# Another order of statements in the step loops of an attention and int8 feed-forward kernel

## The reference

```
x = x + attn(layernorm(x), Wq, Wk, Wv, Wo)
x = x + ffn(layernorm(x), weight, w_scale, bias)

attn: q = rope(x @ Wq); k = rope(x @ Wk); v = x @ Wv
      scores = q k^T / 8, causal; out = softmax(scores) v; out @ Wo
ffn:  scale = max(|x|)/127 per token; q = round(x/scale)
      (q @ weight^T) * scale * w_scale + bias, as float16
```

## Time and profile before

| | us |
|---|---|
| median of 3 runs | 748.71 |
| lowest and highest run | 747.67, 748.79 |
| the profiled execution | 747.3 |
| its span | 745.1 |
| PE busy, PE's weight loads busy | 702.5, 588.8 |
| VectorE, ScalarE, GpSimd busy | 658.8, 634.4, 557.9 |
| mean granted clock of TensorE | 0.992 of full |

### The profile page before, as it was taken

The page is one execution under the profiler, slowest core; times in us unless marked ns, Lnnn a source line. Parts: engine busy times, 40 slices in busy tenths (PEclk is TensorE's granted clock), DMA queues, the critical chain, the costliest instruction groups (busy, mean ns, idle before and its releaser), DMA issues.

```text
span 745.1 us, 22980 instructions
## 1 busy us (share of the span) xinstructions
PE 702.5 (94%) x8014; PEld 588.8 (79%) x8014; DVE 658.8 (88%) x1697; ACT 634.4 (85%) x1317; POOL 557.9 (75%) x525
## 2 busy tenths in 40 slices
PE   4889999999999999999999999999999999999993
PEld 3667887878888888888888888888888888888872
DVE  6858999998889989888899898988989988988996
ACT  4778998888889989898889889898898889888883
POOL 4585887787878898787797798778697898777502
PEclk9999999999999999999999999999999999999996
DMA  8233343343334433333333343333433333232300
GB/s 266 57 98 102 73 118 87 83 114 86 87 87 97 85 92 78 87 92 82 86 92 92 94 96 80 87 90 81 96 85 97 87 94 87 67 71 62 86 2 29
DMA packets 56992, 65.80 MB, mean 88 GB/s; under 512 B 12592, under 2 KB 43824, under 8 KB 56880
## 3 DMA queue, kind: packets, MB, share of 16 engines
q1 hardware_dynamic: 53808, 53.85, 30.1%
q0 software_dynamic: 3072, 10.49, 5.1%
HBM read 16.06 MB, written 2.10 MB: 24 GB/s over the span
## 4 chain that ended last, share of the span: by engine, by line
PE 76%; DVE 11%; ACT 8%; issue 3%; DMA 1%; POOL 0%; ACTq 0%; POOLq 0%; DVEq 0%
PE x_bank L644 23%; PE t_bank L788 19%; PE o_bank L807 13%; PE s_bank L767 7%; PE s_bank L768 6%; ACT prob L1098 5%; DVE neg_max L1465 3%; DVE s_bank L1473 2%; PE ot_bank L858 2%; DVE probT L1453 2%; PE s_bank L773 2%; PE t_bank L644 1%; ACT neg_max L1096 1%; DVE value_lo L1323 1%; ACT probT L989 1%
## 5 line engine op out<-in xcount | busy, mean ns | idle before, releaser
L1110 ACT ACTIVATE probT<-t_bank 128x512 f16<-128x512 f32 x320 | 192.1, 600 | 46.3 <-PE t_bank L788 46.3
L1453 DVE SCALAR_TENSOR_TENSOR probT<-t_bank,probT 128x512 f16<-128x512 f32 x320 | 215.2, 686 | 13.5 <-ACT probT L1110 11.4
L788 PE MATMUL t_bank<-ident,prob 128*128 128x128 f32 x1280 | 192.1, 277 | 1.1 <-DVE value_lo L1323 0.7
L1473 DVE CUSTOM_DVE_ANT_0 s_bank<-s_bank,mask_row,score_unit 128x512 f32<-128x512 f32 (+1 forms) x256 | 174.6, 683 | 3.5 <-PE s_bank L768 1.8
L807 PE MATMUL o_bank<-value_hi,probT 128*128 128x65 f16 x2560 | 157.8, 194 | 5.1 <-DVE probT L1453 3.3
L1098 ACT ACTIVATE prob<-s_bank,neg_max 128x512 f32<-128x512 f32 (+1 forms) x256 | 161.2, 645 | 1.2 <-DVE neg_max L1473 1.0
L807 PEld LDWEIGHTS o_bank<-value_hi,probT 128*128 128x128 f16 x2560 | 137.7, 97 | 25.9 <-DVE probT L1453 18.6
L788 PEld LDWEIGHTS t_bank<-ident,prob 128*128 128x128 f32 x1280 | 144.0, 141 | 15.3 <-issue 2.3
L767 PE MATMUL s_bank<-kT,qT 128*128 128x384 f16 (+3 forms) x512 | 140.4, 301 | 11.1 <-ACT prob L1098 7.5
L807 PE MATMUL o_bank<-value_lo,probT 128*128 128x64 f16 x1280 | 141.7, 192 | 0.0
L768 PE MATMUL s_bank<-kT,qT 128*128 128x384 f16 (+3 forms) x512 | 139.3, 299 | 0.0
(11 more groups left out here) (146 smaller groups left out, 1151.3 us busy)
## 6 DMA issues: line engine op xcount, KB each, us to landing
...
qT<-query_pair SPq DMA_DIRECT2D x256, 64.0 KB, 2.1
kT<-key_pair SPq DMA_DIRECT2D x128, 64.0 KB, 2.0
...
```

The source lines that it names most:

```text
L788: last = nc.tensor.transpose(t_bank[B % TURN_BANKS][:, h * P:(h + 1) * P], prob[:, B % PROBS, h, :], ident[:, :])
L1110: nc.scalar.activation(turned_half[B % TURNED][HI], t_bank[B % TURN_BANKS][:, :], ACT.Copy, scale=PROB_SCALE).then_inc(probT_hi, 1)
L1453: nc.vector.scalar_tensor_tensor(out=turned_half[B % TURNED][LO], in0=t_bank[B % TURN_BANKS][:, :], scalar=PROB_SCALE, in1=turned_half[B % ...
L1473: nc.vector.tensor_tensor_reduce(bank, bank, mask_row[:, SEQ - n:SEQ], score_unit[:, 1, s % KV_HEADS:s % KV_HEADS + 1], UNBOUNDED, ALU.add ...
```

## The change

The same statements stand in another order in the step loops of the five engines. The arguments of each, the number of instructions, tiles, buffers and semaphores are the same. On SyncE the queries of pair 1 are placed before those of pair 0, the loads of output weights stand between them, and stores stand before place_keys. GpSimd rotates and loads in another order. On PE scores(s, 10) stands before turn(s, 4), attend(s, 2) behind turn(s, 5), turn(s, 7) before turn_output(s, 1). On ScalarE keep_high(s + 1, 1) stands later, and keep_raw(s + 2, 0) and keep_probT(s, 6) are exchanged with their neighbours. On VectorE several statements of the middle and the feed-forward part move.

```diff
--- before.py
+++ after.py
@@ -384,18 +384,18 @@
             swap_halves(1, 1)
             for s in range(STEPS):
                 swap_key_halves(s + 2)
+                if s == WO_CHUNKS:
+                    load_ffn_rows()
+                place_queries(s + 1, 1)
                 if s % 2 == 0:
                     load_wo(s + 2)
                     load_wo(s + 3)
                 place_queries(s + 1, 0)
-                place_queries(s + 1, 1)
                 swap_halves(s + 2, 0)
                 swap_halves(s + 2, 1)
-                if s == WO_CHUNKS:
-                    load_ffn_rows()
-                place_keys(s + 2)
                 for f in biased_tiles(s - 1):
                     store_tile(f)
+                place_keys(s + 2)
 
             for f in biased_tiles(STEPS - 1):
                 store_tile(f)
@@ -595,26 +595,26 @@
                 rotate_second(s + 1, 1)
                 rotate_first(s + 1, 1)
                 rotate_sum(s + 1, 1)
+                scale_inputs(scaled_tiles(s))
                 keep_low(s + 1, 0)
                 keep_low(s + 1, 1)
+                rotate_keys_first(s + 2)
                 done_rstd(s)
+                rotate_keys_second(s + 2)
+                split_group_weights(s + 3)
+                rotate_keys_sum(s + 2)
                 for f in biased_tiles(s):
                     add_bias(f)
                     add_residual(f)
-                split_group_weights(s + 3)
-                scale_inputs(scaled_tiles(s))
                 if s % 2 == 1:
                     keep_wo_low(s + 1)
                     keep_wo_low(s + 2)
-                rotate_keys_second(s + 2)
-                rotate_keys_first(s + 2)
-                load_group_weights(s + 5)
-                rotate_keys_sum(s + 2)
-                keep_keys_low(s + 2)
                 for f in normalised_tiles(s):
                     normalise_done(f)
+                keep_keys_low(s + 2)
+                rotate_first(s + 2, 0)
                 rotate_second(s + 2, 0)
-                rotate_first(s + 2, 0)
+                load_group_weights(s + 5)
                 rotate_sum(s + 2, 0)
 
             normalise_done(LOOP_TILES)
@@ -914,35 +914,35 @@
             for s in range(STEPS + 1):
                 turn(s, 0)
                 scores(s, 4)
+                sum_next_weights(s)
                 turn_output(s - 1, 3)
-                sum_next_weights(s)
                 project_keys(s + 2)
                 scores(s, 5)
                 scores(s, 6)
                 attend(s, 0)
                 turn(s, 1)
+                turn_quant(done_tile(s))
                 turn(s, 2)
-                turn_quant(done_tile(s))
                 scores(s, 7)
                 out_product(s - 1, 3)
                 turn_output(s, 0)
                 scores(s, 8)
                 turn(s, 3)
                 attend(s, 1)
+                ffn_product(done_tile(s))
                 scores(s, 9)
-                ffn_product(done_tile(s))
+                scores(s, 10)
                 turn(s, 4)
-                attend(s, 2)
-                scores(s, 10)
                 project(s + 2, 0)
                 turn(s, 5)
+                attend(s, 2)
                 attend(s, 3)
+                turn(s, 6)
                 attend(s, 4)
-                turn(s, 6)
                 out_product(s, 0)
+                turn(s, 7)
                 turn_output(s, 1)
                 attend(s, 5)
-                turn(s, 7)
                 attend(s, 6)
                 turn(s, 8)
                 out_product(s, 1)
@@ -1196,10 +1196,12 @@
                 exponentials(s, 1, 1)
                 keep_probT(s, 0)
                 exponentials(s, 1, 2)
+                keep_oT(s - 1, 3)
+                exponentials(s, 1, 3)
                 if s % 2 == 1:
                     keep_wo(s + 1)
-                keep_oT(s - 1, 3)
-                exponentials(s, 1, 3)
+                if s % 2 == 1:
+                    keep_wo(s + 2)
                 keep_raw_keys(s + 2)
                 keep_high(s + 1, 0)
                 keep_probT(s, 1)
@@ -1207,22 +1209,20 @@
                 keep_probT(s, 2)
                 exponentials(s, 2, 1)
                 keep_oT(s, 0)
-                keep_high(s + 1, 1)
                 exponentials(s, 2, 2)
                 keep_probT(s, 3)
+                keep_high(s + 1, 1)
                 exponentials(s, 2, 3)
                 keep_probT(s, 4)
                 exponentials(s, 3, 0)
                 exponentials(s, 3, 1)
+                keep_probT(s, 5)
                 keep_raw(s + 2, 0)
-                keep_probT(s, 5)
+                keep_probT(s, 6)
                 exponentials(s, 3, 2)
-                keep_probT(s, 6)
                 exponentials(s, 3, 3)
                 keep_oT(s, 1)
                 keep_probT(s, 7)
-                if s % 2 == 1:
-                    keep_wo(s + 2)
                 round_tile(done_tile(s + 1))
                 keep_probT(s, 8)
                 to_whole(done_tile(s + 1))
@@ -1230,10 +1230,10 @@
                 keep_high_keys(s + 2)
                 keep_raw(s + 2, 1)
                 keep_oT(s, 2)
+                for h in range(GROUP_HEADS):
+                    exponentials(s + 1, 0, h)
                 if s == STEPS - 1:
                     root(2, slice(LOOP_TILES, LOOP_TILES + 2))
-                for h in range(GROUP_HEADS):
-                    exponentials(s + 1, 0, h)
 
             normalise_done(LOOP_TILES + 1)
             root(3, slice(LOOP_TILES + 2, TOK_TILES))
@@ -1585,62 +1585,62 @@
             for s in range(STEPS + 1):
                 if s < STEPS:
                     normalise_output(s - 1, 3)
+                batch_statistics(s, 0)
                 maxima(s, 3)
-                maxima(s, 4)
                 if s % KV_HEADS == 2:
                     for f in maximum_tiles(s):
                         absolute_maximum(f)
+                maxima(s, 4)
                 group_scales(s + 2, o_bank, 0)
                 keep_probT_low(s, 0)
+                batch_statistics(s, 1)
                 keep_oT_low(s - 1, 3)
                 maxima(s, 5)
                 invert_sums(s, 0)
                 maxima(s, 6)
+                keep_quant(done_tile(s))
                 normalise_output(s, 0)
-                keep_quant(done_tile(s))
-                batch_statistics(s, 0)
+                keep_probT_low(s, 1)
                 if s == STEPS:
                     finish_root(2, slice(LOOP_TILES, LOOP_TILES + 2))
                     offset_means(2, slice(LOOP_TILES + 1, LOOP_TILES + 2))
-                keep_probT_low(s, 1)
                 maxima(s, 7)
+                add_product(s - 1, 3)
                 keep_probT_low(s, 2)
-                add_product(s - 1, 3)
                 maxima(s, 8)
-                maxima(s, 9)
-                batch_statistics(s, 1)
                 batch_statistics(s, 2)
                 scale_product(done_tile(s))
+                maxima(s, 9)
                 keep_probT_low(s, 3)
+                batch_statistics(s, 3)
+                group_maxima(s + 3)
                 keep_probT_low(s, 4)
+                keep_oT_low(s, 0)
                 maxima(s, 10)
-                group_maxima(s + 3)
-                keep_oT_low(s, 0)
-                batch_statistics(s, 3)
+                keep_probT_low(s, 5)
                 invert_sums(s, 1)
                 normalise_output(s, 1)
-                keep_probT_low(s, 5)
-                invert_scales(scaled_tiles(s))
                 keep_probT_low(s, 6)
                 add_product(s, 0)
+                batch_aggregate(s)
+                invert_scales(scaled_tiles(s))
                 keep_oT_low(s, 1)
                 keep_probT_low(s, 7)
-                last_statistics(s, 0)
-                batch_aggregate(s)
                 add_product(s, 1)
                 invert_sums(s, 2)
+                keep_probT_low(s, 8)
                 normalise_output(s, 2)
                 if s % KV_HEADS == 3:
                     for f in maximum_tiles(s):
                         absolute_maximum(f)
-                keep_probT_low(s, 8)
                 keep_probT_low(s, 9)
                 maxima(s + 1, 0)
+                last_statistics(s, 0)
                 keep_oT_low(s, 2)
-                last_statistics(s, 1)
                 maxima(s + 1, 1)
                 invert_sums(s, 3)
                 maxima(s + 1, 2)
+                last_statistics(s, 1)
                 if s == STEPS - 1:
                     normalise_output(s, 3)
                     aggregate(LOOP_TILES, LOOP_TILES + 2, TOK_TILES)
```

## The result

| | before | after |
|---|---|---|
| median of 7 runs each, us | 748.51 | 751.05 |
| lowest and highest | 747.67, 748.98 | 750.25, 751.76 |
| ratio, 95% interval | | 1.0034 [1.0023, 1.0046] |
| the profiled execution, its span | 747.3, 745.1 | 750.7, 748.8 |

The changed kernel is 2.5 us slower, a third of a percent: above the 0.2% that a measurement can tell. The forecast, no change at 748.9 us, has the time within its range and the side wrong; "slower" had a chance of 0.29. Three runs among those behind this document, of 1006 and 2463 us (the kernel before) and 3964 us (a variant), stand far outside the rest and are in no ratio or median.

The account below looks back on a forecast made before the run. TensorE was taken to bound the kernel, with little wait in reach; steps +0.3, batch steps +0.3, step 0 +0.3 and early steps -0.5 gave about +0.4 us, stated as 748.9 us on a median of 748.71, range 744.5 to 753.0.

Parts of the forecast that it names:

- What bounds the kernel, and how much can change: TensorE bounds it, with some 40 us of load waits; the order reaches only a small wait in a step's middle.
- waits for probT "near 17" us: Sign of a right forecast: TensorE's waits for VectorE's low halves of turned probabilities stay near 17 us.
- The sum: Steps +0.3, batch steps +0.3, step 0 +0.3, early steps -0.5: about +0.4 us, given as 748.9 us.
- The middle of step 17: From scores(s,9) to attend(s,7): TensorE gains 0.10 us, lost again before out_product(s,1) with 0.03 on top.
- Steps: 32 x (0.00 to 0.03) = 0 to +1.0 us, taken as +0.3: All 32 steps: each keeps its length or grows by up to 0.03 us through the oT chain before out_product(s,1).
- the slower rival: oT chain slips 0.15 us more per step before out_product(s,1), if keep_oT starts after 429.75: 4.8 us, 753.5; chance 0.24.
- The faster rival: oT chain keeps up, so TensorE keeps its 0.10 to 0.17 us a step: 3.5 us, 745.2 us; chance 0.28.
- Early steps' out_product(s,0), whose oT half comes sooner, -0.5: In the early steps out_product(s,0) gets its oT half sooner, gaining 0.5 us.
- Step 0, +0.3: Step 0, already late with its queries, may wait once, 0 to 1 us, taken as +0.3.
- Batch steps, +0.3: Steps 8, 16, 24: aggregation before keep_oT_low(s,1) costs at most 0.37 us each; +0.3 us in all.
- GpSimd ... free: GpSimd's key and query rotations move by up to a microsecond at no cost, since it idles and has 0% of the chain.
- The late-queries rival: Query transfers landing over 4.9 us after issue cost 0.5 us in each of 16 even steps: 8 us, 757; chance 0.05.

Follow-up runs that it names:

- the run with the order turned round: Changed kernel with core engines in former order in the last two steps, plus keep_oT_low(s,1) ahead of batch_aggregate and invert_scales on VectorE; 750.13 us, 1.0025.
- the three core lists: TensorE, ScalarE and VectorE in the changed order, SyncE and GpSimd as in the kernel before; 749.71 us, 1.0026.
- the former ScalarE list: Kernel before with only SyncE's and GpSimd's lists changed, TensorE, ScalarE and VectorE as before; 749.23 us, 1.0010.

## Why the prediction was right and wrong

**What bounds the kernel, and how much can change: right.** The waits at the start and the end of a step are the same to 0.01 us in step 17 (0.68, 0.51 and 0.35 against the earlier trace rows), the time stayed within the range, and the gap before attend(s,5) is gone. One sign contradicted the text's own count: waits for probT "near 17" us cannot stand beside a gap of 0.17 us that goes in each of 32 steps, 5.4 us; 11.3 was measured. Step lengths "within 0.05 us" became 0.065.

**The sum** is added up wrongly at its end: +0.4 on a median of 748.71 is 749.1, not 748.9.

**The middle of step 17: right in every link, short by 0.05 us.** From the step's start:

| | computed | measured |
|---|---|---|
| turn(s,4) | 7.23 | 7.24 |
| turn(s,5) | 9.10 | 9.07 |
| turn(s,6) | 10.26 | 10.22 |
| out_product(s,0) | 11.06 | 11.05 |
| turn_output(s,1) | 12.25 | 12.28 |
| keep_oT(s,1) | 12.65 | 12.70 |
| low half | 13.16 | 13.21 |
| out_product(s,1) | 13.70 | 13.75 |

The kernel before has the last at 13.67, and the text says "with 0.03 on top": measured 0.08, of which the step keeps 0.065. The terms that were short lie on TensorE: turn(s,7) to turn_output(s,1), taken as 0.39 as if a float32 product followed, is 0.43 (430.52 to 430.95); turn(s,6) to attend(s,4), taken as 0.44, is 0.47; and the 0.04 us that keep_oT(s,1) needs behind its input were left out, as ScalarE was taken to be the later of the two. The scaling, the two exponentials and the copy behind keep_probT(s,6), taken as 1.72 up to keep_oT, are just that where keep_oT doesn't wait (10.89 to 12.61 with turn_output(s,1) back); in the full change it waits for turn_output until 12.70. A few hundredths each, in a sum of which the answer was three hundredths. That the wait before out_product(s,1) is there is seen in the trace; no run here took its 0.065 us a step back, since each move that loosened this chain made another wait.

**"Steps: 32 x (0.00 to 0.03) = 0 to +1.0 us, taken as +0.3": the term that failed first.** It is 0.065 us in each of twenty steps, 1.30 us in these alone, past the upper end. It is the mechanism of the slower rival (turn_output(s,1) behind turn(s,7)) at under half its size: keep_oT(s,1) at 12.70, where I had put the point of decision at 429.75, 12.72. The faster rival, PE keeping its 0.10, was there in PE's count and fell as the forecast said.

**"Early steps' out_product(s,0), whose oT half comes sooner, -0.5": did not come**; steps 0 to 5 are +0.09 in all. In step 1 the product had waited for that half (11.76 of the step); after, the half is 0.9 us sooner and TensorE is at the product at 11.81, later than before. In step 5 it hadn't waited. **Step 0, +0.3: +0.01. Batch steps, +0.3:** 0.41, or 0.22 above what every step has; 0.08 us in each of the three is the aggregation ahead of keep_oT_low(s,1), which makes up the 0.22, but the run with the order turned round shows that the other place costs more. Step 11 came 0.16 shorter, which nothing in the text foresaw; the three core lists show it too (21.05). Why is open.

**The last two steps: missing from the text, 1.15 us of 2.8.** I laid out one step and multiplied by 32. The two steps without a projection have another middle, and the prediction named project(s+2,0) as what stands between turn(s,4) and turn(s,5) without asking where it isn't. This alone would have moved the forecast from 749.1 to about 750.3, the edge of what counts as slower.

**"GpSimd ... free": right for the full change**, whose early steps are as long as before, with ScalarE's new place for keep_high as the likely cover; with the former ScalarE list steps 0 to 5 took 1.15 us more in the one trace. **The queries** were in time: in the odd steps they have 1.4 to 2.6 us to spare before scores(s+1,0), the forecast 1.2 to 2.9. In steps 0, 2 and 4 it is 0.5 to 0.7, in step 30 0.25, which the text, laid out on step 17, doesn't have. The late-queries rival did not arise.

Of the two rules weighed there, the Trainium skill, Perfetto Trace Analysis, Identifying the Most-Contended Engine, judges the headroom of TensorE by MFU (the matmul work done against the peak) or by the busy share of LDWEIGHTS; by the second that is an estimate of 157 us. No order tried here won any of it, and none won any of the 40 us of gaps either, so these runs don't decide between the two.
